# Score rows six steps ahead of the columns in a causal attention kernel, with the turnings of the maxima moved to the ends of steps

## The reference

```
Q, K, V = heads(layernorm(x))
scores  = Q K' / 4 + lambda * (tanh(Q) J) tanh(K)'      # one product of width 32 per head
scores  = where(j > i, -inf, scores)
x       = x + (softmax(scores) V) Wo' + bo
```

## Time and profile before

| what | before |
|---|---|
| median of 3 runs | 2140.23 us (2136.8 to 2142.74) |
| profiled execution | 2137.79 us |
| its span, first to last instruction | 2136.1 us |
| PE busy | 1957.2 us, 92% |
| DVE busy | 1246.5 us, 58% |
| ACT busy | 1065.7 us, 50% |
| POOL busy | 820.6 us, 38% |
| attention, from the first columns to the last | about 87 to 1146 us |

### The profile page before, as it was taken

How to read it: one execution, slowest core, us unless ns; L and a number is a source line. 1 busy time by engine, 2 the same in 40 slices (tenths; PEclk the granted TensorE clock), 3 DMA queues, 4 the chain that set the end, 5 groups by cost and what they waited for, 6 DMA issues and landing times. The chain is left out here.

```text
span 2136.1 us, 48445 instructions
## 1 busy us (share of the span) xinstructions
PE 1957.2 (92%) x14755; PEld 1296.5 (61%) x14824; DVE 1246.5 (58%) x3875; ACT 1065.7 (50%) x2310; POOL 820.6 (38%) x1206
## 2 busy tenths in 40 slices
PE   2689999999999999999988999997999999999997
PEld 1345445454454544545435788886777777777776
DVE  5666667766667666776662865553445545444553
ACT  1255555555555555555552345452555555555553
POOL 4033323333323333233332037773444444444443
PEclk9799999999999999999999999999999999999999
DMA  7234443344443434434322346654863333333332
GB/s 240 60 106 117 121 136 124 110 118 119 136 130 107 122 111 140 128 114 124 100 87 79 137 134 226 223 188 150 215 167 58 57 55 55 56 55 57 54 57 34
DMA packets 156641, 246.08 MB, mean 115 GB/s; under 512 B 29408, under 2 KB 90592, under 8 KB 156480
## 3 DMA queue, kind: packets, MB, share of 16 engines
q1 hardware_dynamic: 120960, 189.24, 28.9%
q0 software_dynamic: 32064, 53.44, 12.2%
q10 hardware_dynamic: 3456, 1.34, 0.3%
HBM read 111.89 MB, written 90.50 MB: 95 GB/s over the span
## 5 line engine op out<-in xcount | busy, mean ns | idle before, releaser
L680 DVE CUSTOM_DVE_ANT_0 ps_rows<-ps_rows,maskrow 128x128 f32<-128x128 f32 (+1 forms) x1009 | 477.1, 514 | 290.9 <-PE ps_rows L525 282.2
L623 ACT ACTIVATE probs<-ps_cols 128x512 f32<-128x512 f32 (+3 forms) x1024 | 392.0, 435 | 386.7 <-PE ps_cols L536 380.1
L525 PE MATMUL ps_rows<-ks,qs 32*128 32x512 f32 x1984 | 403.1, 480 | 73.5 <-DVE mx L680 38.6
L532 PE MATMUL ps_cols<-qs,ks 32*128 32x512 f32 (+3 forms) x2048 | 418.5, 485 | 2.5 <-ACT probs L623 2.4
L1642 POOL DMA_INDIRECT out_dram<-y_e,to x135 | 216.1, 1601 | 349.4 <-DMA out_dram<-y_e,to 221.5
L799 POOL TENSOR_TENSOR pace<-eps 1x1 f32<-1x1 f32 x256 | 58.2, 227 | 747.0 <-ACT probs L623 747.0
L525 PEld LDWEIGHTS ps_rows<-ks,qs 32*128 32x128 f32 x1984 | 153.3, 184 | 268.5 <-DVE mx L680 221.9
L536 PE MATMUL ps_cols<-mT,ones_r 32*128 32x512 f32 (+3 forms) x1024 | 284.8, 550 | 0.0
L1771 DVE TENSOR_TENSOR h_lo<-ps_h,h_hi 128x512 fp32r<-128x512 f32 x135 | 93.3, 691 | 232.6 <-ACT h_hi L1746 232.6
L1740 ACT ACTIVATE sg_e<-ps_ge 128x512 f32<-128x512 f32 x135 | 80.7, 598 | 263.1 <-PE ps_ge L1664 261.0
L554 PE MATMUL ps_o<-probs,vt 128*32 128x512 f32 (+3 forms) x2048 | 192.5, 448 | 0.8 <-POOL probs L801 0.8
(11 more groups left out here) (220 smaller groups left out, 3838.9 us busy)
## 6 DMA issues: line engine op xcount, KB each, us to landing
xs_d<-zrows SPq DMA_DIRECT2D x45, 408.0 KB, 2.9
xr<-xs_d POOLq DMA_DIRECT2D x135, 136.0 KB, 3.3
whi_d<-w_sh SPq DMA_DIRECT2D x16, 768.0 KB, 3.8
w_hi<-whi_d SPq DMA_DIRECT2D x24, 512.0 KB
xn<-in_L_attn_x_dram SPq DMA_DIRECT2D x16, 512.0 KB, 5.2
ks<-k_lin SPq DMA_DIRECT2D x64, 128.0 KB, 3.0
ks<-k_tan SPq DMA_DIRECT2D x64, 128.0 KB, 3.7
qs<-q_lin SPq DMA_DIRECT2D x64, 128.0 KB, 2.4
```

The source lines that it names most:

```text
L525: mm = nc.tensor.matmul(ps_rows[bank_of(row_no(g, it, h))][:, 0:(it + 1) * P], qs[at:at + STRIP, d.par, g, it * P:(it + 1) * P], ks[at:at ...
L532: nc.tensor.matmul(ps_cols[bank_of(col_no(n, s, e))][:, jt * P:S], ks[at:at + STRIP, b.par, gc, jt * P:(jt + 1) * P], qs[at:at + STRIP, b. ...
L623: nc.scalar.activation(probs[:, n % 2, 2 * (1 - s) + e, jt * P:S], ps_cols[bank_of(col_no(n, s, e))][:, jt * P:S], ACT.Exp).then_inc(exp_d ...
L680: nc.vector.tensor_tensor_reduce(out=bank, in0=bank, in1=maskrow[:, (TT - 1 - it) * P:S], scale=1.0, scalar=LOWEST, op0=ALU.add, op1=ALU.m ...
```

## The change

`LEAD` goes from 8 to 6. With 8, a multiple of four, rows and columns of a step have the same width; with 6 they are two blocks apart: columns of 512, 384, 256 and 128 stand beside rows of 256, 128, 512 and 384. Rows of a batch begin in step 10 of the batch before and not in step 8. The four turnings `mt` move: from step 1, place 0 (between the halves) to step 2, place 1; from step 5 to 6 and from 9 to 10, both place 1; and from step 14, place 0 to step 14, place 1. `first_rows` ends with the rows that the prologue now forms: six steps of them, not eight.

```
-LEAD = 8
+LEAD = 6
...
     (0, 0, "xt", 0, 1), (0, 1, "xt", 1, 1),
-    (1, 0, "mt", 1, 0),
-    (2, 0, "k", 0, 1),
+    (2, 0, "k", 0, 1), (2, 1, "mt", 1, 0),
     (3, 0, "k", 1, 1),
     (4, 0, "q", 0, 1),
-    (5, 0, "q", 1, 1), (5, 1, "mt", 2, 0),
-    (6, 0, "qj", 0, 1),
+    (5, 0, "q", 1, 1),
+    (6, 0, "qj", 0, 1), (6, 1, "mt", 2, 0),
     (7, 0, "qj", 1, 1),
     (8, 0, "v", 0, 1),
-    (9, 0, "v", 1, 1), (9, 1, "mt", 3, 0),
-    (10, 0, "out", 0, -1),
+    (9, 0, "v", 1, 1),
+    (10, 0, "out", 0, -1), (10, 1, "mt", 3, 0),
...
-    (14, 0, "mt", 0, 1),
+    (14, 1, "mt", 0, 1),
...
-        return d.off == 0 and u < STEPS * HG // 2
+        return d.off == 0 and u < LEAD * HG
```

## The result

The changed kernel takes 2260.99 us (median of 4 runs, 2254.95 to 2264.32) against 2141.48 before: 1.0566 times as long, 95% interval 1.0539 to 1.0592. The forecast was 2236, range 2192 to 2265, so slower as forecast and 25 us slower than the likeliest case. The profiled execution took 2258.70 us (span 2257.0), 120.9 more than that of before.

A forecast was written before the change was run, and what follows sets the result against it. PE was taken as the bound: 61.6 us of work a batch plus 5.3 added and 6.4 of waits, 73.3 (+6.8). Fifteen batches 102, last batch 1.6, prologue -7: +97, forecast 2236 us, range 2192 to 2265.

The forecast's parts named there:

- C: Half with columns 256 wide beside rows 512 wide: PE work rises from 0.76 to 1.06 us, 0.30 more.
- D: Half with columns 128 wide beside rows 384 wide: PE work rises from 0.49 to 0.85 us, 0.36 more.
- Rival 2: Strips share PE, so a mixed half costs its widths' mean; batch 70.4 us, total about 2190 us; chance 0.07.
- Rival 1: Column passes end only after rows' passes issued ahead; 1.4 us more a batch, 2258 us in all; chance 0.18.
- One wide loop in every half: Every half waits on a 512 or 384 wide exponents' or maxima loop; waits 6.4 us a batch, 1.5 more.
- A: Half with columns 512 wide beside rows 256 wide: PE work 1.30 us, loop 2.05 by exponents.
- B: Half with columns 384 wide beside rows 128 wide: PE work 1.03 us, loop 1.67 by exponents.
- nothing there now: First halves of steps 1 and 14, left without a piece to fill the loop: waits of 0.64 and 1.09 us.
- What moves at no cost: New turning places, DMA, POOL and SP counted at zero; late `nm` or `mT` would cost 4.7 us a batch.
- The last batch: Changed in its first half only: 2.6 us of work less about 1 of waits, +1.6.
- Rival 3: Faster: waits behind xT and for exponents go, 2.6 us less a batch, 2094 us; chance 0.05 with lesser gains.
- Rival 4: DVE takes over in steps 9 to 11: three halves lose 0.4 us each, 2254 us in all; chance 0.08.

The follow-up runs named there:

- wide6: Changed kernel with row products computed as wide as the wider columns beside them (256 to 512, 128 to 384), extra scores thrown away: 2225.62 us.
- mix8: Kernel before, lead of eight and old turnings kept, with only the row blocks reordered so that widths in a step are unequal: 2259.82 us.
- match6: Changed kernel, lead of six and new turnings kept, with row blocks reordered so that rows and columns are equally wide again: 2188.38 us.
- turn8: Changed kernel's table with the lead set back to eight, so only the turnings' new places differ from the kernel before: 2167.16 us.
- norm6: Changed kernel with DVE's layer norm moved from the end of step 9 to the end of step 12: 2243.31 us.
- tail8: Kernel before with second xT piece and group 1 turning exchanged, plus unread row products on idle strips in the last batch's steps 9 to 15: 2128.88 us.
- wide4: Changed kernel with row products widened to the columns' width only in steps 12, 13, 0 and 1: 2230.96 us.
- gaps6: Changed kernel with group 0's turning back between the halves of step 14 and the second xT piece moved from step 0 to step 1: 2237.57 us.

## Why the prediction was right, and where it was short

**A mixed half lasts as its wider side: right.** C and D were forecast at 1.06 and 0.85 and are 1.06 and 0.85. Rival 2 (shared strips) asked for 0.95 and 0.68 and falls; wide6 shows it from the other side, where wider rows beside wide columns cost 0.25 us a batch and not 3. Mixed widths alone (mix8) make a loss as large as the change, and with equal widths (match6) 73 us of the loss go.

**Rival 1 (passes end in order) falls.** It asked for 1.18 and 0.91. In the C half above, the ones of the column strips begin at 657.34 and end at 657.81, the rows' second pass, issued for products ahead of them in the program, runs from 657.51 to 658.10 (ends are modelled; the starts alone show it). The Trainium skill's rule that matmuls start and end strictly in order (TensorE: Matmul & The Clock Gate, Part 3, The mechanism) does not hold here for the passes of fp32 products on different strips; the trace decides.

**One wide loop in every half: right.** Waits were forecast at 6.4 a batch and are 5.7. Where nothing else fills them, A and B halves last 2.15 and 1.77 us (forecast 2.05 and 1.67, by exponents), C and D 2.10 and 1.75 (2.15 and 1.78, by maxima). Of the places with "nothing there now" step 14 came as worked out (2.10 against 2.15); step 1 was 2.27 and not 1.67, since maxima queue on DVE behind the subtraction for xT, which itself waits 1.17 us for ACT (DVE's timeline):

```profile
611.83 0.69 DVE L698 TENSOR_TENSOR xT<-ps_m,xT 128x512 fp32r<-128x512 f32 x1 [1.17 <-ACT xT L584]
612.44 0.29 DVE L679 CUSTOM_DVE_ANT_0 ps_rows<-ps_rows,maskrow 128x128 f32<-128x128 f32 x1
```

And step 10 was 3.26 and not about 3.5 (2.99 of work with 0.5 of lateness). At full clock a batch is 72.35; I had 73.3.

**"What moves at no cost" was too broad.** That `nm` and `mT` are in time is right: no wait for them shows. But turn8 shows 1.93 us a batch for the places alone. At mixed widths most of this was in the sum, as empty gaps in steps 1 and 14; the lateness of step 10 was sized at 0.5 and measured 0.27 there (norm6), 0.54 at equal widths. Its cause was another than forecast: not the wider maxima behind the layer norm (mix8 has them and is not late) but the turning that no longer covers it.

**The prologue and the last batch.** The prologue was forecast at -7 and measured -8.1, in part by luck: the other five kernels with a lead of six have their first columns at 78.1 to 85.9 us, against 79.1, with the same pieces in the prologue taking longer in the late ones (the first `q` piece 2.93 us in wide6, 1.65 here). The last batch was mis-sized. Its +1.6 took waits to fall, but no pieces of a next batch stand there to fill the loops of its C and D halves. Steps 2 and 3 of the last batch, from first row product to that of step 4, before and after:

```profile
1092.70 0.48 PE L525 MATMUL ps_rows<-ks,qs 32*128 32x256 f32 x2
...
1097.77 0.70 PE L525 MATMUL ps_rows<-ks,qs 32*128 32x512 f32 x2
```

```profile
1200.73 0.70 PE L524 MATMUL ps_rows<-ks,qs 32*128 32x512 f32 x2
...
1208.76 0.48 PE L524 MATMUL ps_rows<-ks,qs 32*128 32x256 f32 x2 [0.27 <-DVE mx L679]
```

That is 8.03 us against 5.07, in one of two such places; the whole batch loses about 5 at full clock (62.95 to the last `pv` in wide6, 57.56 in tail8, neither with a fall in it).

**The other rivals.** **Rival 3 (faster)** fell as argued: the waits behind xT went, and C's and D's work was several times that. **Rival 4** asked for 0.4 in each of three halves of steps 9 to 11; those are as in the table but for the 0.3 above.

**The term that is missing is the clock.** The sum took every duration at full clock. Measured: sixteen of the 93 us of thirteen batches, and about 11 in batch 0 (17.3 against 6 for a batch). Behind batch 14, of 18.6 us, 5.7 are batch 14, about 5 the last batch and 1.2 what comes after the last `pv`; the other 6 or so fit the 27.3 us at 1.2 GHz there, 13.7 before. That is about 34 in all. wide6 shows it: from the first columns to the end its profiled execution takes 36 us less than the changed kernel's, without making a batch shorter. My batch was 1 us too long, 15 us in all, and hid part of this in the forecast; that the time lies in the range, 4 us below its upper bound, is so far luck.

Why the clock falls is not shown. In this kernel filling the thin strips stops the falls at the same waits (wide6, wide4). But thin strips are neither enough for a fall nor needed for one, as the windows view of mix8, gaps6 and match6 shows:

```profile
330.00:1226.00 896.00, 809.29 (x6852) 394.35 (x6844) 538.25 (x1980) 446.35 (x1044) 256.39 (x548) 1.00 0.36 108
```

```profile
190.00:1180.00 990.00, 919.32 (x7784) 450.22 (x7783) 605.72 (x2249) 508.45 (x1184) 292.46 (x621) 1.00 0.37 112
```

```profile
320.00:1210.00 890.00, 791.87 (x7084) 422.05 (x7083) 551.89 (x2008) 450.70 (x1069) 275.59 (x572) 0.98 0.37 111
```

mix8 and gaps6 have the thin strips and keep the clock at full speed in these stretches. match6 has equal widths, and its clock falls in seven of the batches 2 to 12, each time in step 14 behind PE's longest wait, as here, where the turning already takes 1.12 us and not 0.66:

```profile
633.48 0.48 PE L525 MATMUL ps_rows<-ks,qs 32*128 32x256 f32 x2 [1.64 <-DVE mx L680]
...
635.07 1.12 PE L463 MATMUL ps_m<-ident,nm 128*128 128x128 f32 x4
```

PE's longest wait in the thirteen batches is 1.2 us in the changed kernel and norm6, whose clock falls in step 1 behind it. In the stretches above it is 1.0 in mix8 (its one fall in the thirteen batches, at 315.7 us, stands behind one of 1.03) and 0.8 in gaps6, where the second xT piece fills the gap of step 1. With equal widths turn8 has a wait of 1.4 and no fall. So in these traces the falls went when the strips were filled, and also when the gap was; how the two act together stays open.

## What to carry to other kernels

Where products run on separate strips, pair equal widths: the narrower one is free, the wider one is paid, so the sum over pairs of the wider width is the cost to look at, not the sum of columns. Pairing wide with narrow to even out the load of two other engines gives each step one wide loop and none that is short. A small piece of work is worth what the gap under it leaves: before moving one, ask which late engine it was covering, and after a change that thins out PE's work or lengthens a wait look at the granted clock before believing a sum at full clock.

## What the runs showed of the hardware that was not expected

Adding products made a kernel faster: 2225.62 us with rows widened on strips that would have run empty, 2260.99 without. The granted clock fell to 1.2 GHz in stretches where PE was busy for 4.73 of 6.10 us with half-empty strips, and did not where the same stretch had the same waits and full strips; with full strips it fell too, behind a wait of 1.64 us (match6). And the passes of fp32 products on different strips overtake each other: ones that stand later in the program began 0.17 us ahead of the second pass of rows that stand earlier.
